# A token-mixing and expert kernel: expert biases by adding gathers, and the last step's values made ahead of the expert tiles

## The reference, cut to what matters

```
xn  = layernorm(x)
# branch 1, a recurrence over time per channel
k = xn @ key_w.T;  v = xn @ value_w.T;  r = sigmoid(xn @ recep_w.T)
wkv_t = (e1*aa + e2*v_t) / (e1*bb + e2 + 1e-6)     # the reference's scan
attn  = (r * wkv) @ out_w.T
# branch 2, 8 experts, each token goes to 2
scores = softmax(xn @ gate_w.T + gate_b);  top_w, top_i = top_k(scores, 2)
expert_e(t) = (silu(t@w1e.T + b1e) * (t@w3e.T + b3e)) @ w2e.T + b2e
y = sum over the 2 experts e of a token of  top_w[e] * expert_e(token)
z = silu(xn@ws1.T + bs1) * (xn@ws3.T + bs3) @ ws2.T + bs2     # shared expert
out = x + attn + y + z
```

## Time and profile before

| | us |
|---|---|
| median of 3 runs | 473.65 (469.54 to 474.9) |
| the profiled execution | 470.54 |
| its span, first to last instruction | 468.8 |
| PE busy, share of the span | 95% |
| DVE, ACT, POOL busy | 78%, 51%, 50% |
| stage: until the first expert matmul | 0 to 66.8 |
| stage: expert tiles, until the last down-multiplication | 66.8 to 259.2 |
| stage: mixing | 259.2 to 468.8 |

### The profile page before, as it was taken

How to read it: one execution, slowest core, us unless ns; L and a number is a source line. 1 busy time by engine, 2 the same in 40 slices (tenths; PEclk the granted TensorE clock), 3 DMA queues, 4 the chain that set the end, 5 groups by cost and what they waited for, 6 DMA issues and landing times.

```text
span 468.8 us, 8342 instructions
## 1 busy us (share of the span) xinstructions
PE 445.1 (95%) x2549; PEld 374.1 (80%) x2549; DVE 365.1 (78%) x680; ACT 239.8 (51%) x394; POOL 232.5 (50%) x224
## 2 busy tenths in 40 slices
PE   5898977979999999999998999999999999999997
PEld 4453746858888888888887879798888889898987
DVE  5968868798776987878675689996968687877863
ACT  4778735677768586876754532423324142324031
POOL 3234777354858658589744477661523425160000
PEclk9899769999999999999999999999999999999999
DMA  8999743255674854344454863726152433431001
GB/s 245 396 351 285 211 115 94 66 199 203 237 264 120 273 183 139 125 136 135 119 198 158 290 238 113 251 68 228 50 185 86 155 122 123 157 119 63 25 24 45
DMA packets 45874, 77.24 MB, mean 165 GB/s; under 512 B 5924, under 2 KB 32268, under 8 KB 45836
## 3 DMA queue, kind: packets, MB, share of 16 engines
q1 hardware_dynamic: 36924, 55.83, 33.8%
q0 software_dynamic: 8240, 20.88, 16.9%
q10 hardware_dynamic: 672, 0.04, 0.1%
HBM read 48.52 MB, written 28.21 MB: 164 GB/s over the span
## 4 chain that ended last, share of the span: by engine, by line
PE 46%; POOL 18%; issue 13%; DVE 10%; DMA 4%; ACT 4%; SPq 3%; POOLq 0%; DVEq 0%; ACTq 0%
POOL xg L1005 8%; PE ps_w L1540 5%; PE ps_w L1542 5%; PE ps_w L1541 5%; PE ps_w L1605 5%; PE ps_w L1606 5%; PE ps_w L1607 5%; PE ps_g L1082 4%; DMA w_lo<-w_all 3%; POOL den L1017 2%; PE ps_y L1082 2%; SPq L424 2%; POOL den L1016 2%; DVE stats L687 2%; POOL firsts L1024 2%
## 5 line engine op out<-in xcount | busy, mean ns | idle before, releaser
L1005 POOL DMA_INDIRECT xg<-xn_rows,tile_tok x71 | 71.4, 1006 | 21.9 <-issue 19.1
L1516 POOL DMA_INDIRECT yg<-expert_rows,rows x64 | 66.8, 1044 | 23.6 <-issue 17.1
L1082 PE MATMUL ps_g<-w_hi,x_hi 128*128 x142 | 56.7, 399 | 1.6 <-DVE x_lo L1237 1.6
L1082 PE MATMUL ps_g<-w_lo,x_hi 128*128 x142 | 56.7, 399 | 0.0
L1082 PE MATMUL ps_g<-w_hi,x_lo 128*128 x142 | 56.3, 397 | 0.0
L1647 ACT ACTIVATE sact<-ps_w,vec_b 128x512 f32<-128x512 f32 x32 | 22.0, 687 | 58.7 <-PE ps_w L1542 58.7
L1540 PE MATMUL ps_w<-col_hi,s_hi 128*128 128x512 f32 x128 | 50.5, 395 | 0.4 <-DVE shid L1758 0.4
L1542 PE MATMUL ps_w<-col_hi,s_lo 128*128 128x512 f32 x128 | 50.2, 392 | 0.0
L1541 PE MATMUL ps_w<-col_lo,s_hi 128*128 128x512 f32 x128 | 50.1, 392 | 0.0
L1082 PE MATMUL ps_y<-w_hi,h_hi 128*128 x142 | 43.1, 304 | 1.3 <-DVE h_lo L1253 1.3
L1246 DVE TENSOR_TENSOR hid<-ps_g,act 128x512 f32<-128x512 f32 (+1 forms) x36 | 23.7, 657 | 25.5 <-ACT act L1158 25.5
(11 more groups left out here) (247 smaller groups left out, 1278.5 us busy)
## 6 DMA issues: line engine op xcount, KB each, us to landing
expert_rows<-y SPq DMA_DIRECT2D x35, 256.0 KB, 2.2
w_lo<-w_all SPq DMA_DIRECT2D x16, 384.0 KB, 10.1
table<-mix_tables SPq DMA_DIRECT2D x8, 768.0 KB, 6.7
xT<-x SPq DMA_DIRECT2D x16, 256.0 KB, 6.1
xn_rows<-xn SPq DMA_DIRECT2D x16, 256.0 KB, 9.2
xn_columns<-xT SPq DMA_DIRECT2D x8, 512.0 KB
col<-xn_columns SPq DMA_DIRECT2D x8, 512.0 KB, 5.0
res<-x SPq DMA_DIRECT2D x16, 256.0 KB, 2.9
```

Source lines behind the costliest of these rows:

```text
L1005: pool.indirect_dma_start(out=xg[b][:, t, :], out_offset=None, in_=xn_d[:, :], in_offset=bass.IndirectOffsetOnAxis(ap=tile_tok[:, first_ti ...
L1082: mm = nc.tensor.matmul(out, x[:, k, :], w[:, ds(e, 1), k, cols].rearrange("p o n -> p (o n)"), start=(k == 0 and n == 0), stop=(last and ...
L1516: pool.indirect_dma_start(out=yg[a.buf(2)][:, k, q, :], out_offset=None, in_=y_d[:, :], in_offset=bass.IndirectOffsetOnAxis(ap=picked[a.bu ...
```

## The change

**Biases by gathers.** `terms`, its transposes, `gT`, the bias rows, `low_rows`, `pick` and the bias matmul are removed. DVE keeps the rank of both chosen experts (`rank`) and writes it as the index of a bias row; slots and these indices stand in one table (`picks`). In `mix`, POOL's `prepare(a)` gathers the expert rows as before, waits until they have landed, and gathers the bias row of each onto it with addition. The shared bias, broadcast to all partitions once, is added to the residual by POOL (`add_shared`). DVE's `experts` waits for both.

**Values of the last step.** SP loads the value weights raw (`raw_v`, 256 KB) ahead of the last two weight pieces. After the token lists PE multiplies them in fp32 by the last column tile, which is still in SBUF, and ACT copies the two results to `last_v`. In the last mixing step PE makes no values and DVE reads `last_v`.

**Splitting.** The low parts of weight pieces 4 and 5 are made by DVE instead of PE and ACT (BOTH 6 to 4), and DVE makes six low parts instead of two before the first tile (LOW 2 to 6).

```
@@ route
-        MADE, BOTH, HIGH, LOW = 4, 6, 13, 2
+        MADE, BOTH, HIGH, LOW = 4, 4, 13, 6
@@ sync
                 step(At(0, i, NSTEP))
+            sp.dma_start(raw_v[:], wvr.rearrange("(k p) n -> p k n", p=P)[:, :, 0:C]).then_inc(s_rawv, 16)
             for i in arriving:
                 load_w(i)
@@ gpsimd
-            nc.gpsimd.memset(terms[:], 0.0).then_inc(s_terms, 1)
-            pool.wait_ge(s_terms, 1)
-            nc.gpsimd.memset(terms[:, :, 3 * E:3 * E + 2], 1.0).then_inc(s_terms, 1)
@@ scalar
-            act.wait_ge(s_terms, 3)
-            for n in (0, 2):
-                ins = nc.scalar.activation(terms[:, :, n * E:(n + 1) * E].bitcast(F32R), dense[:], ACT.Copy)
-            ins.then_inc(s_terms, 1)
-            for i in range(4, BOTH):
-                made_lo(act, i)
+            for m in range(KC):
+                act.wait_ge(s_lastmm, m + 1)
+                nc.scalar.activation(last_v[:, m, :], ps_w[2 + m], ACT.Copy).then_inc(s_lastv, 1)
@@ tensor
-            for i in range(4, BOTH):
-                rest(pe, i)
+            pe.wait_ge(s_rawv, 16)
+            pe.wait_ge(s_both, BOTH)
+            for m in range(KC):
+                for k in range(KC):
+                    mm = nc.tensor.matmul(ps_w[2 + m], raw_v[:, k, m * P:(m + 1) * P], xT[NSTEP - 1][:, k, :],
+                                          start=k == 0, stop=k == KC - 1)
+                mm.then_inc(s_lastmm, 1)
@@ vector
-                own.link(nc.vector.tensor_reduce(red[:, t], work2[:, t], AX_X, ALU.max))
-                own.link(nc.vector.tensor_tensor(hot[0][:, t], work2[:, t], wide(red[:, t]), ALU.is_equal))
+                own.link(nc.vector.tensor_reduce(rank[:, 0, t], work2[:, t], AX_X, ALU.max))
+                own.link(nc.vector.tensor_tensor(hot[0][:, t], work2[:, t], wide(rank[:, 0, t]), ALU.is_equal))
...
-            own.link(nc.vector.tensor_copy(tile_exp[:], exp_f[:]))
-            scaled()
-            dve.wait_ge(s_terms, 2)
-            nc.vector.tensor_tensor(dense[:], score, mask[:].rearrange("p e j -> p j e"), ALU.mult).then_inc(s_terms, 1)
+            nc.vector.tensor_copy(tile_exp[:], exp_f[:]).then_inc(s_ready, 1)
+            own.link(nc.vector.reciprocal(gates[:, 0, :], red[:]))
             dve.wait_ge(s_gate, 1)
             nc.vector.tensor_tensor(gates[:, 1, :], gates[:, 1, :], gates[:, 0, :], ALU.mult)
-            dve.wait_ge(s_terms, 4)
-            nc.vector.tensor_tensor(terms[:, :, E:2 * E], dense[:], terms[:, :, 0:E], ALU.subtract
-                                    ).then_inc(s_terms, 1)
+            nc.vector.tensor_scalar(bias_row, rank[:], 1.0, float(E), ALU.max, ALU.min).then_inc(s_ready, 1)
             for i in range(LOW):
                 split_lo(dve, i)
@@ run_experts, tensor
-            pe.wait_ge(s_terms, 5)
-            for i in range(NSTEP):
-                mm = nc.tensor.transpose(ps_y[i // 4][:].rearrange("p t c -> p (t c)")[:, i % 4 * P:(i % 4 + 1) * P],
-                                         terms[:, i * Q:(i + 1) * Q, :].rearrange("p q n -> p (q n)"), ident[:])
-                if i % 4 == 3:
-                    mm.then_inc(c_turn, 1)
+            pe.wait_ge(s_ready, 1)
+            pe.wait_ge(s_lastv, KC)
             es[0] = experts(0)
@@ mix, gpsimd
-                nc.gpsimd.tensor_copy(picked[a.buf(2)][:], slots[:, :, ds(a.i * Q, Q)]).then_inc(b_idx, 1)
+                nc.gpsimd.tensor_copy(picked[a.buf(2)][:], picks[:, :, ds(a.i * Q, Q)]).then_inc(b_idx, 1)
...
-            def pick(a):
-                at_least(pool, b_o, a.i * Q - Q)
-                nc.gpsimd.tensor_copy(g_now[a.buf(2)][:], gT[:, ds(a.i, 1), :].rearrange("p o n -> p (o n)")
-                                      ).then_inc(b_gc, 1)
+            def add_biases(a):
+                pool.wait_ge(b_gath[a.buf(2)], (a.uses(2) + 1) * 16 * TOPK * Q)
+                pool.sem_inc(b_go, 1)
+                for k in range(TOPK):
+                    for q in range(Q):
+                        pool.indirect_dma_start(
+                            out=yg[a.buf(2)][:, k, q, :], out_offset=None, in_=b_all,
+                            in_offset=bass.IndirectOffsetOnAxis(ap=picked[a.buf(2)][:, TOPK + k, q:q + 1], axis=0),
+                            compute_op=ALU.add
+                        ).then_inc(b_rows[a.buf(2)], 16)
+
+            def add_shared(a):
+                pool.wait_ge(b_res[a.buf(2)], (a.uses(2) + 1) * 32)
+                nc.gpsimd.tensor_tensor(res[a.buf(2)][:], res[a.buf(2)][:],
+                                        shared_b[:, None, :].broadcast_to([P, Q, C]), ALU.add).then_inc(b_bias, 1)
+
+            def prepare(a):
+                gather(a)
+                add_biases(a)
+                add_shared(a)
 
             def step(a, first, left):
-                pick(a)
                 if left > 0:
-                    gather(a.plus(1))
+                    prepare(a.plus(1))
...
-            gather(At(0, 0, 2))
-            pool.wait_ge(e_gT, 2)
+            pool.wait_ge(s_ready, 2)
+            pool.wait_ge(e_ld, loaded * 16)
+            prepare(At(0, 0, 2))
@@ mix, tensor
-            def values(a):
+            def values(a, last=False):
                 at_least(pe, b_xlo, a.i)
-                at_least(pe, b_a, a.i * MIX - MIX + 2)
-                for m in range(KC):
-                    mm = columns(ps_v[:, m, :], vr_hi, vr_lo, m * P, x_hi[a.buf(2)], x_lo[a.buf(2)])
-                mm.then_inc(b_v, 1)
+                if not last:
+                    at_least(pe, b_a, a.i * MIX - MIX + 2)
+                    for m in range(KC):
+                        mm = columns(ps_v[:, m, :], vr_hi, vr_lo, m * P, x_hi[a.buf(2)], x_lo[a.buf(2)])
+                    mm.then_inc(b_v, 1)
...
                 def mixed(q):
-                    nc.tensor.matmul(ps_w[q][:, 0:C], g_now[a.buf(2)][:], rows_b[:, q, :],
-                                     start=True, stop=False)
                     for k in range(KC):
                         three_rows(ps_w[q][:, 0:C], a_hi, a_lo, k, slice(q * P, (q + 1) * P), o_hi, o_lo,
-                                   False, False)
+                                   k == 0, False)
@@ mix, vector
-                v = ps_v[:].rearrange("p k (b t) -> p k b t", b=B)
-                dve.wait_ge(b_v, a.i + 1)
+                v = (last_v if last else ps_v)[:].rearrange("p k (b t) -> p k b t", b=B)
+                if last:
+                    dve.wait_ge(s_lastv, KC)
+                else:
+                    dve.wait_ge(b_v, a.i + 1)
...
                 if g == 0:
-                    dve.wait_ge(b_res[buf], (a.uses(2) + 1) * 32)
-                    dve.wait_ge(b_gath[buf], (a.uses(2) + 1) * 16 * TOPK * Q)
+                    dve.wait_ge(b_bias, a.i + 1)
+                    dve.wait_ge(b_rows[buf], (a.uses(2) + 1) * 16 * TOPK * Q)
...
             dve.wait_ge(e_y, DUOS)
+            dve.wait_ge(e_wlo, 2)
@@ kernel, host side
-        "b_all": np.concatenate([get("L0_ffn_b2")] * 3 + [get("L0_ffn_bs2")[None]] * 2, axis=0),
+        "b_all": np.concatenate([get("L0_ffn_bs2")[None], get("L0_ffn_b2")[::-1]], axis=0),
```

More of the change, by code:

```diff
@@ L224, in _, with route @@
                 mix_vector(dve)
-def route(nc, kept, x, first, decay, vec_tf, vec_td, gate_w, gate_b, w_all, w_first, nw_d, xn_d, xT_d, ident, slots, gates,
-          tile_tok, tile_exp, w_hi, w_lo, terms, lane_i, row_of1, minus):
+def route(nc, kept, x, first, decay, vec_tf, vec_td, gate_w, gate_b, w_all, w_first, nw_d, xn_d, xT_d, ident, slots, bias_row, gates,
+          tile_tok, tile_exp, w_hi, w_lo, lane_i, row_of1, minus, wvr, last_v):
     with ExitStack() as ctx:
@@ L353, in route @@
         s_Tout = sem("s_Tout")
-        s_terms = sem("s_terms")
+        s_ready = sem("s_ready")
+        s_rawv = sem("s_rawv")
+        s_lastmm = sem("s_lastmm")
+        s_lastv = sem("s_lastv")
         s_dve = sem("s_dve")
@@ L984, in sync @@
                     sp.dma_start(*loads[a - A_LOADS]).then_inc(c_ld, 16)
-                if a == A_ROWS:
-                    sp.wait_ge(c_zero, 1)
-                    for q in range(Q):
-                        sp.dma_start(rows[TERMS * q:TERMS * q + 3 * E + 2, q, :], b_all).then_inc(c_rows, 16)
                 if a == 4 * LAST_V + 1:
@@ L1194, in scalar @@
             cut_x(0)
-            for h in range(2):
-                act.wait_ge(c_turn, h + 1)
-                nc.scalar.activation(gT[:, 4 * h:4 * h + 4, :].rearrange("p j n -> p (j n)"),
-                                     ps_y[h][:].rearrange("p t c -> p (t c)"), ACT.Copy).then_inc(c_gT, 1)
             silu(0)
@@ L1217, in scalar @@
                     halves(v)
-                if a == A_HI:
-                    act.wait_ge(c_rows, 16 * Q)
-                    act.wait_ge(c_zero, 1)
-                    nc.scalar.activation(rows_hi[:], rows[:], ACT.Copy).then_inc(c_rhi, 1)
                 if a == DUOS - 4:
@@ L1365, in vector, with mix @@
                     differences(v + 1)
```

(18 more changed lines are left out.)

93 lines of the change are left out of this document (23 added, 70 removed).

## The result

The changed kernel took 542.75 us in the median (540.42 to 543.54, 4 runs), the kernel before 471.6 us (469.13 to 474.9, 4 runs). The ratio is 1.150, 95% interval 1.140 to 1.159: slower by 15%. The profiled execution of the changed kernel took 543.54 us around a span of 541.8, against 470.54 and 468.8 before: 73.0 us more, where the forecast had 63.3.

What follows compares the result with a forecast made beforehand. PE bounds the kernel before; with the change POOL bounds mixing at 30.9 us per step (11.9 + 1.86 + 0.3 + 14.4 + 2.4). Step 7 moves from 450.1 to 513.4, so 470.5 + 63.3 = 533.8, forecast 534 us, range 490 to 562.

Steps and rivals of the forecast that it cites:

- from it to step 0 prepared: Start of mixing: from POOL's copy at 262.54, gathers landed at 278.7, adds and shared add done at 295.8.
- seven more preparations: Mixing steps 1 to 7: POOL, never waiting for other engines, takes 30.9 us each and ends at 512.1.
- POOL becomes the bound: Mixing stage: POOL's queue needs 30.9 us per step against a period of 25.4, so all engines become late.
- The price of an add: POOL's mixing steps: an adding gather takes 1.54 us, not the plain 0.954; eight with gaps take 14.4 us.
- the rival of dearer adds: Mixing stage: one 4.06 us add in every eight gives 554 us, or 1.91 us per add gives 558; 12%.
- The landing wait: POOL, between plain and adding gathers: 1.86 us after the last gather's span plus 0.3 us to issue.
- The adds' landing at the end: Last mixing step: the last add lands 5.2 us after its issue, at 513.4.
- The gains of PE counted as zero: Mixing stage: PE sheds 3.8 us of bias and 2.8 us of value multiplications, 6.6 together, counted as zero.
- POOL's work stays hidden, 464: Rival for the mixing stage: adds start below about 0.8 us apart, PE's 6.6 us come through, 464 us; 5%.
- Edits ahead of the tiles at nothing: Before the first expert tile and in the expert stage: all edits together nothing, bounds -2 to +5 us.
- The clock: PE in the mixing stage: perhaps 2 us at 1.2 GHz after each pause, costing 1 of 6 idle us.
- A factor of two for the adding DMA: Rival for POOL's adds: twice the plain price, 1.91 us each, period 33.9, 558 us; within the dearer case's 12%.

Runs made afterwards that it cites:

- e1: The changed kernel without its 64 adding gathers, the experts' biases left out: 470.65 us, ratio 0.9997 to the kernel before.
- e3: The changed kernel with the adding gathers of the first choice alone, four a step instead of eight: 487.86 us, ratio 1.038 to the kernel before.
- e7: The changed kernel with six two-input SBUF operations of DVE in the mixing stage replaced by constant writes: 536.12 us, ratio 1.142 to the kernel before.
- e4: The changed kernel with POOL's shared add moved ahead of the adding gathers, into the landing wait: 529.25 us, ratio 1.129 to the kernel before.
- e6: The changed kernel without adding gathers and without POOL's shared add; DVE waits for the residual's load: 464.91 us, ratio 0.989 to the kernel before.
- e5: The kernel before with only the last step's values made early in fp32 and kept, all biases unchanged: 470.38 us, ratio 0.9994.
- e2: The changed kernel with each adding gather made a plain, overwriting gather of the same bias row: 503.03 us, ratio 1.072 to the kernel before.

## Why the prediction was right, and where its sizes were off

The shift was 73.0 us against 63.3, all from the mechanism that was named; 542.75 lies inside the range of 490 to 562. (A preparation is what POOL does for one step: copy, plain gathers, wait, adds, shared add.)

| term | predicted | in the profile after |
|---|---|---|
| first copy of mixing | 262.54 (edits ahead: 0) | 260.52: -2.0 |
| from it to step 0 prepared | 33.3 | 35.5: +2.2 |
| seven more preparations | 7 x 30.9 | to 522.67, 7 x 32.4: +10.4 |
| landing of the last add behind them | 1.3 | DVE starts at 522.77: -1.2 |
| from there to the end of the span | 18.7 | 19.0: +0.3 |

The terms sum to +9.7, as measured (73.0 - 63.3). Two of them came out well by luck: the -2.0 at the start is scatter, and the -1.2 of the landing hides part of what the preparations took more. In the seven later preparations the adds took 15.7 us in the mean instead of 14.4, the wait 2.8 instead of 2.16, and copy, plain gathers and shared add together 14.0 instead of 14.3.

- **POOL becomes the bound: right.** e1 gives all of the 72 us back, e3 half the adds for 55, and POOL's timeline has no pause but the landing wait and the short gaps ahead of each instruction. The order of the terms showed as predicted: DVE's gate multiplication waits for POOL's shared add (three steps) or for a bias row (five), PE behind it.
- **The price of an add: the plain size was right, the mean was not.** The rows said 1.54, chosen over 0.954 by the packet counts. Of the 64 adds, 18 began while a DVE operation with two inputs in SBUF was running. They took 2.02 us in the mean (16 of them 1.65 to 2.53; the two that met only its last 0.1 us, 1.53). The other 46 took 1.53 to 1.58 (mean 1.54), also the 15 of them that began during an operation of DVE with an input in PSUM. The two rows of DVE that belong to the long adds at 380.15 and 388.22 above:

```profile
379.78 1.22 DVE L1658 TENSOR_TENSOR part_a<-part_a,part_v 128x1024 f32<-128x1024 f32 x1
...
387.68 1.22 DVE L1697 TENSOR_TENSOR col_lo<-col,col_hi 128x1024 fp32r<-128x1024 f32 x1
```

 They end 0.85 and 0.68 us after the add's start, and the add is 0.71 and 0.55 longer than 1.54. The add at 386.39 took 1.53, although such an operation began at 386.54, inside it. e7 took these operations away and with them all long adds. That is the mis-sized step: eight times 0.135, 1.1 us per preparation. With the adds at 1.544, e7 came to 536, close to the 534 forecast, though partly because other errors offset each other: its preparations took 31.6 us, not 30.9.

 The trace of the kernel before had this already. Of its 64 plain gathers in the mixing stage, 29 began during such an operation and took 1.155 us in the mean; the other 35 took 0.94 to 0.97. The prediction priced by medians, which hide it; the mean of the same gathers shows it (1044 ns, the number behind the busy time):

```profile
L1516 POOL DMA_INDIRECT yg<-expert_rows,rows x64 | 66.8, 1044 | 23.6 <-issue 17.1 <-POOL rows L1511 6.5
```

 The Trainium skill ("SBUF — State Buffer", sections "Who interferes with whom" and "Summary: rules for kernel authors") says that a DVE instruction with two SBUF inputs contends with a GpSimd instruction that reads SBUF, and that the second one to issue is blocked until the first finishes. The rows agree in both directions: POOL's gather, whose indices lie in SBUF, waits for DVE here, and DVE's L1701 waited for POOL in e1 (3.34 instead of 1.23 us). Which access of the gather has to wait, no run here shows.

 The add of 4.06 us in the earlier trace rows, from which the rival of dearer adds was priced, began inside a run of two-input operations of DVE too, and ended 1.42 us after the last of them (57.36); but the add at 50.80, which began in such a run as well, took 1.68. What a run of them does to an add is open.
- **The landing wait: too small.** 2.16 us were taken; it was 4.18 in the first step, 3.18 in the second, and mostly 2.6 later (23.6 in eight). In every step the last gather issued is also the last to land. In five of the eight it lands 2.7 to 2.8 us after its start, as was taken; here the one of 370.93:

```profile
L1451 POOL DMA_INDIRECT yg<-expert_rows,rows x1: 950/950/950, 370.9 to 370.9; - x1
...
DMA to landing us min/median/max: 2.8/2.8/2.8
```

 That is 373.7, and the first add starts at 374.48. Here lies the error in those steps: the first add starts 0.8 to 0.9 us after the landing that it waited for, not the 0.3 us that lie between two gathers. The first gather of a step, which waits for the copy, has the same 0.8 us (361.83 above). In the first, second and last step the landing was slower as well: 4.3, 4.0 and 3.4 us. All this is worth 2.0 us ahead of step 0 and 0.6 in each later preparation; e4, which fills the wait, came out 13.5 us shorter.
- **The adds' landing at the end: too large.** I took 5.2 us from adds under a busy DMA; here the median was 4.2, most of it beside the shared add.
- **The gains of PE counted as zero: right for this kernel, for the reason given.** They exist (e6, 5.3 of 6.6 us), and POOL's bound hides them. What the prediction missed is that even without that bound they would not have come: the shared add alone takes them back through DVE (e1 against e6, 1.1% of the time). The rival "POOL's work stays hidden, 464" could thus not have come true at any price of an add: with no adds at all, e1 ended at about 470.
- **Edits ahead of the tiles at nothing: right within the scatter.** The first copy of mixing stood between 260.0 and 264.4 in the seven traces that share the changed early part, 262.54 before, and e5 shows that the fp32 values by themselves cost nothing there.
- **The clock.** It was 0.50 for some 3 us of work behind a pause, where 2 us had been guessed; PE had the time to spare, as predicted.
- **A factor of two for the adding DMA**, the rival's 1.91 us, did not show: 1.54 against 0.95 us, 1.6 times. The Trainium skill ("Collectives: The Full Stack", section "The bandwidth ceiling: the fold count and why AG ≠ RS ≠ AR"), from which that factor was read, counts read descriptors; the measured time decides here.

## What to carry to other kernels

Before work is moved to an engine with a low busy share, add up its queue in the stage where it lands, with the issue gaps and waits that "busy" does not count: POOL was 50% busy and 13 us free per step, and was given 20. An indirect DMA with addition is not priced like the plain one of the same bytes: 1.54 against 0.95 us for 128 rows of 1 KB here, and packets per byte in the queue's counts told so before. Price an instruction that comes 64 times by its mean and look at the long ones: the median (0.954 us) hid the gathers that waited for DVE (mean 1.044). An elementwise operation on POOL beside two-input operations of DVE can cost the bound engine as much as the work that it saves.

## What the runs showed of the hardware that was not expected

- A gather on POOL that starts during a two-input SBUF operation of DVE is held until this ends (adds of up to 2.53 us in place of 1.54). The 15 adds that began during an operation with an input in PSUM were not held: 1.53 to 1.58 us. One that is already running is not lengthened by a two-input operation that begins inside it: 11 such adds, 1.545 us in the mean. The five plain gathers of e7 that were held from a constant write on remain unexplained.
- On POOL an indirect DMA starts 0.3 us after the one before it, but 0.8 to 0.9 us after a copy or a landing that it waited for.
- The other way round, DVE's operation waits for POOL's: 3.34 instead of 1.23 us and 2.76 instead of 0.68 us beside POOL's shared add of 2.4 us.
- An adding gather moves 144 packets per 128 rows of 1 KB, a plain one 48, whatever the source rows (e2 and the changed kernel read the same ones).
